# Sending the row maxima from ScalarE's queue, and storing the last chunk in two parts

## The chip, the cores and the metric

The kernel runs on one core of a Trainium2 chip. The metric is the device time of one execution in microseconds (us), lower is better. The engines are called PE (TensorE, matmul), PEld (TensorE's weight load), ACT (ScalarE), DVE (VectorE), POOL (GpSimd) and SP (SyncE). A name with q behind it (SPq, ACTq) stands for an instruction that the engine's own sequencer carries out, such as the issue of a DMA.

## The reference

One sequence of 2048 tokens by 256 features goes through three sublayers. The first and the third are the same attention with 16 heads of 16 features: the queries have 16 heads, but keys and values are those of the one head that a gate picks for each token.

```python
def _L0_ffn_ref(x, W_gate, W_qkv):              # T = 2048, C = 256, H = 16, hd = 16
    gating = softmax(x @ W_gate.T);  idx = argmax(gating)
    indicator = one_hot(idx, H);     gating_top1 = indicator * max(gating)
    q, k, v = split(x @ W_qkv.T, 3)             # k, v as (T, H, hd)
    k_shared = einsum('bth,bthd->btd', indicator, k)
    v_shared = einsum('bth,bthd->btd', gating_top1, v)
    att = einsum('bhqd,bkd->bhqk', q, k_shared) / sqrt(hd)
    att = softmax(where(causal, att, -inf))
    return einsum('bhqk,bkd->bhqd', att, v_shared)
...
x = x + 0.5 * _L0_ffn_ref(_layernorm(x), W_gate, W_qkv)
x = x + recurrence(_layernorm(x))               # gates, a scan over tokens, two projections
x = x + 0.5 * _L0_ffn_ref(_layernorm(x), W_gate, W_qkv)
```

## The kernel before

The tokens are cut into 4 chunks of 512 (QW). An attention sublayer (l = 0 or 1) works on units (l, c, g): one chunk of queries and one group of 4 heads, so 32 units in all. Layer 1 takes its chunks in the order 1, 2, 0, 3. A unit goes over its key tiles of 128 keys; a pair (unit, key tile) is a step.

Before a unit's scores can be made, each query needs the maximum of its scores. PE makes score matmuls for that alone ("max" items, line 1724), and DVE reduces them to mxp (lines 1445 and 1448), in some cases after a relu on ACT (line 1217). DVE joins the maxima into mx2 ("join"). The item "row" then has three parts: PE turns mx2 into rows (line 1715), ACT copies these rows from PSUM to the tile m_row (32 x 128, line 1136), and two DMAs take m_row into two extra rows of the query tile q_t, one for the heads of each parity (line 891). There the maximum is subtracted within the score matmul itself, since the keys have a constant in the matching rows. There are two slots of m_row, with a semaphore s_md for each. The first score matmul of a unit ("qk", line 1746) waits for both DMAs.

A step then is: two pairs of score matmuls on PE ("qk"), an exponential on ACT for each pair (line 1229, 128 x 1024 elements, PSUM to the tile probs), a causal mask on POOL for the diagonal tiles (line 971), and the product with the values on PE ("pv", line 1758). After a unit's last step ACT copies the sums (o_sb, line 1237), PE transposes them (line 1733), DVE divides (lines 1472 and 1476) and POOL adds the result to x_sb (line 977, semaphore s_xa). PSUM has 8 banks; a qk pair takes two, a max item one, a unit's sums one.

What each engine does, and in which order, is one static list ORDER. The function weave makes it from a planner's costs before the program is built, and every engine walks through that list and takes the items that are its own. An engine carries out its items strictly in order; semaphores hold it back where data or a bank isn't ready. Short filler matmuls ("warm", lines 1562 and 1565) are in PE's list where the planner saw a gap.

SP issues the DMAs in the same order of items: "qout" (queries to DRAM, line 868), "qin" (queries back in another layout, line 880), "row" (line 891) and "out" (the store of a finished chunk of layer 1, line 897).

Of the kernel before, what the change touches and what calls it, by code (L numbers as in the profile page):

```python
# [6 lines left out]
D = 256  # L7
# [3 lines left out]
P = 128  # L11
EPS = 1e-5
NT = T // P
QW = 512
NCH = T // QW
TC = QW // P
GH = 4
NG = H // GH
# [27 lines left out]
ROWS_M = [slice(HALF * par + KX, HALF * par + KX + 2) for par in range(2)]  # L46
# [13 lines left out]
UNITS = [(0, c, g) for c in range(NCH) for g in range(NG)] \  # L60
# [172 lines left out]
def unit_no(l, c, g):  # L233
    return UNITS.index((l, c, g))
# [327 lines left out]
FREED, _count = {}, {True: 0, False: 0}  # L562
# [30 lines left out]
def fine(l, c):  # L593

    return (l, c) not in SINGLE
# [5 lines left out]
def exp_no(s, k):  # L601

    return PER_STEP * s + k + 1


def filled(e):
    return FILL_NO[e] + 1


def prep_no(l, c):  # L610
    return NO["keys", l, c]


def macaron_block(nc, x, gamma, beta, w_in, b_in, w_out, b_out, w_skip, b_skip, w_gate, w_qkv, out):
# [6 lines left out]
    with ctx:  # L621
        def sb(name, shape, dt=f32):
            return ctx.enter_context(nc.sbuf_tensor(name, shape, dt))
# [4 lines left out]
        def sem(name):  # L628
            return ctx.enter_context(nc.semaphore(name))
# [88 lines left out]
        q_t = sb("q_t", [P, NCH, DC, GH * QW], f16)  # L718
# [4 lines left out]
        m_row = sb("m_row", [2 * GH * TC, 2, P], f16)  # L723
# [27 lines left out]
        def bank_of(e):  # L751
            return ps[:, BANK[e], :]
# [6 lines left out]
        def as_rows(bank):  # L759
            return bank[0:2 * GH * TC, 0:P // 2].bitcast(f16)  # L760
# [9 lines left out]
        s_md = [sem(f"s_md{i}") for i in range(2)]  # L770
        s_out = sem("s_out")
# [3 lines left out]
        s_ra = sem("s_ra")  # L775

        s_qk = sem("s_qk")
# [4 lines left out]
        s_xa = sem("s_xa")  # L782
# [38 lines left out]
        def bands(c):  # L821
            return x_sb[:, TC * c:TC * c + TC, :]
# [16 lines left out]
        def scores_done(u):  # L839

            return exp_no(LAST[u], PER_STEP - 1)

        @block.sync
        def _(sp):
            sp.dma_start(bands(0)[:, 0:2, :], x[0, 0:2 * P, :].rearrange("(t p) d -> p t d", p=P)).then_inc(s_xld[0], 16)

            sp.wait_ge(s_wqkv, 32)
            for c in range(1, NCH):
                sp.dma_start(bands(c), x[0, c * QW:(c + 1) * QW, :].rearrange("(t p) d -> p t d", p=P))\
                    .then_inc(s_xld[c], 16)  # L850
            sp.dma_start(gamma_c[:, :], gamma.rearrange("(a p) -> p a", p=P),
                         allow_slow_non_contiguous=True).then_inc(s_wcol, 16)
            sp.dma_start(beta_c[:, :], beta.rearrange("(a p) -> p a", p=P),
                         allow_slow_non_contiguous=True).then_inc(s_wcol, 16)
            sp.dma_start(b_in_c[:, :], b_in.rearrange("(a p) -> p a", p=P),
                         allow_slow_non_contiguous=True).then_inc(s_wcol, 16)
            sp.dma_start(w_in_sb[:, :, :], w_in.rearrange("(a p) e -> p a e", p=P)).then_inc(s_wbr, 16)
            sp.dma_start(w_skip_sb[:, :, :], w_skip.rearrange("(a p) e -> p a e", p=P)).then_inc(s_wbr, 16)
            sp.dma_start(w_out_sb[:, :], w_out).then_inc(s_wbr, 16)
            sp.dma_start(b_out_r[:, :], b_out.partition_broadcast(P)).then_inc(s_wrow, 16)  # L860
            sp.dma_start(b_skip_r[:, :], b_skip.partition_broadcast(P)).then_inc(s_wrow, 16)

            for e in ORDER:
                if e[0] == "qout":
                    _, l, c, b = e
                    n = prep_no(l, c)
                    sp.wait_ge(s_rd, FREED["q", l, c, b])
                    sp.dma_start(q_scratch[n, :, b].rearrange("a p t -> p a t"), q_part[:, :, b, :])\
                        .then_inc(s_qw[b], 16)
                elif e[0] == "qin":  # L870
                    _, l, c, b = e
                    n = prep_no(l, c)
                    sp.wait_ge(s_qw[b], 16 * (n + 1))
                    if l:

                        sp.wait_ge(s_qk, scores_done(unit_no(0, c, 2 * b + 1)))
                    for par in range(2):
                        for r, part in enumerate(Q_PART):
                            row = HALF * par + HD * r
                            sp.dma_start(  # L880
                                q_t[row:row + HD, c, b, :].rearrange("p (h t) -> p h t", t=QW),
                                q_scratch[n, part, b].rearrange("(h o d) t -> o d h t", o=2, d=HD)[par],
                            ).then_inc(s_qt[n][b], 16)
                elif e[0] == "row":
                    l, c, g = UNITS[e[1]]
                    sp.wait_ge(s_ra, FREED[e])
                    if l:
                        sp.wait_ge(s_qk, scores_done(unit_no(0, c, g)))
                    for par in range(2):
                        o = g % 2 * 2 * QW  # L890
                        sp.dma_start(q_t[ROWS_M[par], c, g // 2, o:o + 2 * QW],
                                     m_row[GH * TC * par:GH * TC * par + GH * TC, e[1] % 2, :])\
                            .then_inc(s_md[e[1] % 2], 16)
                elif e[0] == "out":
                    c = e[1]
                    sp.wait_ge(s_xa, unit_no(1, c, NG - 1) + 1)
                    sp.dma_start(out[0, c * QW:(c + 1) * QW, :].rearrange("(t p) d -> p t d", p=P),
                                 bands(c)).then_inc(s_out, 16)
            sp.wait_ge(s_out, 16 * NCH)

        @block.gpsimd
        def _(pool):
# [16 lines left out]
            def stats_of(e):  # L919
                _, l, c = e  # L920
                k = NO[e]
                pool.wait_ge(s_var, k + 1)
                if k:

                    pool.wait_ge(s_ln, k)
                own(g_.tensor_tensor(rstd[:, :], var[:, :], half[:, 0:TC], op=ALU.pow))  # L926
                g_.tensor_tensor(shift[:, :], neg[:, :], rstd[:, :], op=ALU.mult).then_inc(s_std, 1)

            def norm(e):
                _, l, c = e  # L930
                k = NO[e]
                pool.wait_ge(s_std, k + 1)
                if k:

                    pool.wait_ge(s_fill, filled(TURNS[k - 1]))
                for t in range(TC):
                    last = g_.tensor_scalar(u[:, t, :], x_sb[:, TC * c + t, :], rstd[:, t:t + 1], shift[:, t:t + 1],  # L937
                                            ALU.mult, ALU.add)
                last.then_inc(s_ln, 1)
# [165 lines left out]
        def _(act):  # L1105
# [6 lines left out]
            def evict(e):  # L1112

                bank = bank_of(e)
                act.wait_ge(s_fill, filled(e))
                if e[0] == "wgate":
                    a_.activation(wg_t[:, :, :], bank[:, 0:DC * H].rearrange("p (a h) -> p a h", a=DC), ACT.Copy)\
                        .then_inc(s_ra, 1)
                elif e[0] == "turn" and fine(e[1], e[2]):
                    dst = u2t_x if e[1] == 2 else ut_x  # L1120
                    a_.activation(dst[:, e[3], :, :].rearrange("p a t -> p (a t)"), bank[:, :].bitcast(f16), ACT.Copy)\
                        .then_inc(s_ra, 1)
                elif e[0] == "turn":
                    a_.activation(ut[:, e[3], :], bank[:, :], ACT.Copy).then_inc(s_ra, 1)
                elif e[0] == "keys":
                    _, l, c = e
                    a_.activation(k_tl[:, l, c, :], bank[:, 0:QW // 2].bitcast(f16), ACT.Copy).then_inc(s_ra, 1)  # L1127
                elif e[0] == "dkeys":
                    to = (kd_tl if e[2] else kh_tl)[:, e[1], :]
                    n = to.shape[1]  # L1130
                    a_.activation(to, bank[:, 0:n // 2].bitcast(f16), ACT.Copy).then_inc(s_ra, 1)
                elif e[0] == "row":
                    v = e[1]
                    if v >= 2:
                        act.wait_ge(s_md[v % 2], 32 * (v // 2))
                    a_.activation(m_row[:, v % 2, :], as_rows(bank), ACT.Copy).then_inc(s_ra, 1)

            def preparation(e):
                kind, l, c = e[0], e[1], e[2]
# [668 lines left out]
```

## Time and profile before

| | |
|---|---|
| median of 2 runs | 888.76 us (886.53 to 891.0) |
| profiled execution, its own time | 891.59 us |
| its span, first to last instruction | 889.9 us |
| PE, DVE, ACT, POOL busy | 95%, 84%, 81%, 33% of the span |
| mean granted clock of TensorE | 0.974 of full speed |
| row DMAs (line 891) | 64, of 4.0 KB each |
| chunk stores (line 897) | 4, of 512 KB each, 2.9 us from issue to landing |

The 1.69 us between the profiled execution's own time and its span lie before the first and behind the last instruction. An idle share of an engine says little here by itself, since the engines hand work to each other in one static order.

### The profile page before, as it was taken

Reading aid. Unit: us, or ns where it says so; the run is one execution under the profiler, and the core shown is the slowest. Engines: PE = TensorE matmul, PEld = TensorE weight load, DVE = VectorE, ACT = ScalarE, POOL = GpSimd, SP = SyncE. Lnnn points to the kernel's source line nnn. Section 1 sums busy time; section 2 is a strip of 40 time slices with the busy share of each in tenths; the row PEclk is TensorE's granted clock in tenths of the full one; section 3 lists DMA queues with packets and bytes.
Section 4 is the critical chain, followed back from the end, with each engine's and each line's share of the span. In section 5 each row is a group of like instructions: output and inputs, shape, how many; then the busy total and the mean of one; then the engine's idle time right before and its main releaser. Section 6 shows DMA issues by size and latency. Waiting matters only on the chain.

```text
span 889.9 us, 19042 instructions
## 1 busy us (share of the span) xinstructions
PE 844.8 (95%) x6460; PEld 291.6 (33%) x6460; DVE 747.1 (84%) x2379; ACT 720.6 (81%) x1169; POOL 295.7 (33%) x568
## 2 busy tenths in 40 slices
PE   9898999999999999999999999999999999999997
PEld 6433423332222332324233433342223323222221
DVE  5898778999999989887945889999998999999920
ACT  1148677868998788888979887889998788999996
POOL 3225404633104415046355445632113424110110
PEclk9899689999999999999999999999999999999999
DMA  6110000110000000100010002000001000000000
GB/s 189 49 43 19 2 2 5 57 43 20 1 2 2 1 1 1 43 18 3 1 53 9 2 2 61 3 1 26 1 1 39 25 25 3 24 3 1 2 1 24
DMA packets 20256, 18.03 MB, mean 20 GB/s; under 512 B 4144, under 2 KB 20160, under 8 KB 20160
## 3 DMA queue, kind: packets, MB, share of 16 engines
q1 hardware_dynamic: 19072, 15.74, 5.8%
q8 instruction: 53, 0.87, 0.4%
q10 hardware_dynamic: 1088, 1.07, 0.4%
q14 instruction: 43, 0.35, 0.1%
HBM read 10.24 MB, written 6.29 MB: 19 GB/s over the span
## 4 chain that ended last, share of the span: by engine, by line
PE 59%; DVE 18%; issue 9%; ACT 9%; POOL 5%; DMA 0%; POOLq 0%; SPq 0%; ACTq 0%; DVEq 0%
PE ps L1758 20%; PE ps L1724 12%; PE ps L1746 11%; DVE ps L1448 7%; DVE mxp L1445 5%; ACT probs L1229 5%; PE ps L1642 3%; ACT relu L1217 2%; PE ps L1690 2%; DVE mxp L1448 2%; PE ps L1657 2%; PE ps L1647 2%; PE ps L1565 1%; POOL u L937 1%; POOL u_x L986 1%
## 5 line engine op out<-in xcount | busy, mean ns | idle before, releaser
L1229 ACT ACTIVATE probs<-ps 128x1024 f32<-128x1024 f32 (+5 forms) x802 | 554.9, 767 | 81.2 <-PE ps L1746 76.3
L1758 PE MATMUL ps<-probs,v_l 128*32 128x512 f32 (+3 forms) x2560 | 301.9, 549 | 2.9 <-DVE mxp L1445 0.6
L1448 DVE CUSTOM_DVE_ANT_0 ps<-ps,mask 128x384 f32<-128x384 f32 (+3 forms) x512 | 234.2, 524 | 28.7 <-PE ps L1724 26.7
L1746 PE MATMUL ps<-q_t,k_tl 50*128 50x512 f16 (+3 forms) x1280 | 240.0, 356 | 14.4 <-ACT probs L1229 3.9
L1445 DVE TENSOR_REDUCE mxp<-ps 128x1 f32<-128x512 f32 x384 | 240.2, 683 | 12.7 <-PE ps L1724 10.1
L1724 PE MATMUL ps<-k_tl,q_t 48*128 48x512 f16 (+3 forms) x1152 | 239.4, 340 | 6.9 <-ACT k_tl L1127 1.9
L971 POOL TENSOR_SCALAR_AFFINE_SELECT probs<-probs 128x256 f32<-128x256 f32 x256 | 102.1, 411 | 396.4 <-ACT probs L1229 394.6
L1448 DVE CUSTOM_DVE_ANT_0 ps<-ps,relu 128x256 f32<-128x256 f32 (+1 forms) x256 | 136.1, 586 | 16.3 <-PE ps L1724 15.4
L1724 PEld LDWEIGHTS ps<-k_tl,q_t 48*128 48x128 f16 x1152 | 74.8, 95 | 158.9 <-DVE mxp L1445 48.1
L1746 PEld LDWEIGHTS ps<-q_t,k_tl 50*128 50x128 f16 x1280 | 65.6, 94 | 182.3 <-ACT probs L1229 85.3
L1217 ACT ACTIVATE relu<-ps 128x512 f32<-128x512 f32 x192 | 106.8, 621 | 5.7 <-PE ps L1724 5.2
L1448 DVE DVE_READ_ACCUMULATOR2_ANT mxp<- 128x1 f32 x768 | 108.0, 141 | 0.0
L1758 PEld LDWEIGHTS ps<-probs,v_l 128*32 128x32 f32 x2560 | 53.0, 108 | 86.2 <-issue 69.4
L999 POOL TENSOR_TENSOR prod<-prod 128x512 f32<-128x512 f32 (+2 forms) x42 | 34.5, 821 | 19.3 <-DVE prod L1408 17.1
L1472 DVE RECIPROCAL rec<-ps 128x16 f32<-128x16 f32 x32 | 8.0, 251 | 36.2 <-PE ps L1733 34.8
L1724 PE MATMUL ps<-kd_tl,q_t 48*128 48x512 f16 x128 | 36.3, 382 | 1.6 <-DVE gd L1381 0.5
L977 POOL TENSOR_TENSOR x_sb<-x_sb,y_att 128x256 f32<-128x256 f32 x32 | 23.3, 729 | 43.4 <-DVE y_att L1476 43.3
L1642 PE MATMUL ps<-wqkv_x,ut_x 128*128 128x512 f16 x144 | 34.6, 380 | 0.0
L926 POOL TENSOR_TENSOR rstd<-var,half 128x4 f32<-128x4 f32 x12 | 12.5, 1038 | 59.9 <-DVE neg L1293 59.9
L1408 DVE TENSOR_TENSOR prod<-ps,pick 128x512 f32<-128x512 f32 x32 | 21.9, 687 | 7.1 <-PE ps L1642 5.6
L937 POOL TENSOR_SCALAR u<-x_sb,rstd,shift 128x256 f32<-128x256 f32 x48 | 26.0, 559 | 1.1
L986 POOL TENSOR_TENSOR u_x<-u,u_x 128x512 f16<-128x512 f32 x20 | 23.2, 1160 | 1.7
(182 smaller groups left out, 633.2 us busy)
## 6 DMA issues: line engine op xcount, KB each, us to landing
q_t<-q_scratch SPq DMA_DIRECT2D x96, 64.0 KB, 2.2
q_scratch<-q_part SPq DMA_DIRECT2D x16, 256.0 KB, 2.2
out_dram<-x_sb SPq DMA_DIRECT2D x4, 512.0 KB, 2.9
x_sb<-in_L_attn_x_dram SPq DMA_DIRECT2D x3, 512.0 KB, 5.1
q_t<-m_row SPq DMA_DIRECT2D x64, 4.0 KB
wqkv_n<-in_L_ffn_W_qkv_dram ACTq DMA_DIRECT2D x1, 768.0 KB, 5.5
w_in_sb<-in_L_attn_W_in_dram SPq DMA_DIRECT2D x1, 384.0 KB, 5.5
x_sb<-in_L_attn_x_dram ACTq DMA_DIRECT2D x1, 256.0 KB, 3.5
```

The lines of the kernel that those rows point to most:

```text
L937: last = g_.tensor_scalar(u[:, t, :], x_sb[:, TC * c + t, :], rstd[:, t:t + 1], shift[:, t:t + 1], ALU.mult, ALU.add)
L971: g_.affine_select(out=pr, in_=pr, compare_op=ALU.is_ge, fill=0.0, base=0, pattern=[[0, 2], [1, P]], channel_multiplier=-1).then_inc(s_msk, 1)
L986: g_.tensor_tensor(u_x[:, 1, :, dc * P:(dc + 1) * P], whole, first, op=ALU.subtract).then_inc(s_half, 1)
L999: own(g_.tensor_tensor(pairs[:, :, 0:m], pairs[:, :, 0:m], pairs[:, :, m:2 * m], op=ALU.add))
L1217: a_.activation(relu[:, n % RELU_BUFS, :], bank_of(e), ACT.Relu).then_inc(s_ra, 1)
L1229: last = a_.activation(out if len(banks) == 1 else out[:, n:n + 1, :], bank[:, :, P * i:QW], ACT.Exp, scale=SCALE / LIFT ** 2)
L1445: last = v_.tensor_reduce(to, scores, axis=AX, op=ALU.max)
L1448: last = v_.tensor_tensor_reduce(scores, scores, added, 1.0, LOWEST, ALU.add, ALU.max, accum_out=to)
L1642: last = mm(bank[:, :], ut_x[:, dc, a, t * P:(t + 1) * P], wqkv_x[:, b, dc, D:3 * D], start=n == 0, stop=n == 3 * DC - 1)
L1724: last = mm(bank[:, col:col + w], q_rows(ROWS_X, c, g, hh, i * P, P), keys, start=True, stop=True)
L1746: last = mm(ps[:, BANK[e][n], P * i:QW], k_cols(ROWS_XM, hh, l, kt, P), q_rows(ROWS_XM, c, g, hh, P * i, QW - P * i), start=True, stop=True)
L1758: last = mm(out_bank[VW * hh:VW * hh + VW, P * i:QW], v_l[:, l, kt, :], probs[:, s % NB, hh, P * i:QW], start=j == 0, stop=j == key_tiles( ...
```

## The change

Two things change. First, the row DMAs leave SP's list: ACT, right after its copy into m_row, waits for that copy to be complete (s_ra) and in layer 1 for the layer-0 scores of the same chunk and heads (s_qk), and issues the same two DMAs itself. Second, the store of the last chunk goes out in two DMAs: columns 0 to 191 once the third group of heads has been added, columns 192 to 255 once the fourth has. The other three stores stay whole. ORDER and every other instruction stay the same.

```diff
-                elif e[0] == "row":
-                    l, c, g = UNITS[e[1]]
-                    sp.wait_ge(s_ra, FREED[e])
-                    if l:
-                        sp.wait_ge(s_qk, scores_done(unit_no(0, c, g)))
-                    for par in range(2):
-                        o = g % 2 * 2 * QW
-                        sp.dma_start(q_t[ROWS_M[par], c, g // 2, o:o + 2 * QW],
-                                     m_row[GH * TC * par:GH * TC * par + GH * TC, e[1] % 2, :])\
-                            .then_inc(s_md[e[1] % 2], 16)
                 elif e[0] == "out":
+
                     c = e[1]
-                    sp.wait_ge(s_xa, unit_no(1, c, NG - 1) + 1)
-                    sp.dma_start(out[0, c * QW:(c + 1) * QW, :].rearrange("(t p) d -> p t d", p=P),
-                                 bands(c)).then_inc(s_out, 16)
-            sp.wait_ge(s_out, 16 * NCH)
+                    w = D // NG
+                    for cols in [slice(0, D)] if c != UNITS[-1][1] else [slice(0, D - w), slice(D - w, D)]:
+                        sp.wait_ge(s_xa, unit_no(1, c, cols.stop // w - 1) + 1)
+                        sp.dma_start(out[0, c * QW:(c + 1) * QW, cols].rearrange("(t p) d -> p t d", p=P),
+                                     bands(c)[:, :, cols]).then_inc(s_out, 16)
+            sp.wait_ge(s_out, 16 * (NCH + 1))
...
                     a_.activation(m_row[:, v % 2, :], as_rows(bank), ACT.Copy).then_inc(s_ra, 1)
+                    l, c, g = UNITS[v]
+                    act.wait_ge(s_ra, FREED[e])
+                    if l:
+                        act.wait_ge(s_qk, scores_done(unit_no(0, c, g)))
+                    for par in range(2):
+                        o = g % 2 * 2 * QW
+                        act.dma_start(q_t[ROWS_M[par], c, g // 2, o:o + 2 * QW],
+                                      m_row[GH * TC * par:GH * TC * par + GH * TC, v % 2, :])\
+                            .then_inc(s_md[v % 2], 16)
```

On ACT, around the last of the 32 rows, this stood before (probs are the exponentials, o_sb the sums of the unit before):

```order
L1229 ACTIVATE probs<-ps 128x1024 x18
L1136 ACTIVATE m_row<-ps 32x128
L1229 ACTIVATE probs<-ps 128x1024 x2
L1229 ACTIVATE probs<-ps 128x512 x2
L1229 ACTIVATE probs<-ps 128x1024 x2
L1237 ACTIVATE o_sb<-ps 128x512
```

And this stands there now; the line numbers of later code have moved by two, those of the row by seven:

```order
L1231 ACTIVATE probs<-ps 128x1024 x18
L1129 ACTIVATE m_row<-ps 32x128
L1136 DMA q_t<-m_row 2x8x128 x2
L1231 ACTIVATE probs<-ps 128x1024 x2
L1231 ACTIVATE probs<-ps 128x512 x2
L1231 ACTIVATE probs<-ps 128x1024 x2
L1239 ACTIVATE o_sb<-ps 128x512
```

The two DMAs stand between the copy and the next exponentials, and so it is at all 32 rows.

At the end of SP's list this stood before:

```order
L891 DMA q_t<-m_row 2x8x128 x4
L897 DMA out_dram<-x_sb 128x4x256
L891 DMA q_t<-m_row 2x8x128 x2
L897 DMA out_dram<-x_sb 128x4x256
L891 DMA q_t<-m_row 2x8x128 x6
L897 DMA out_dram<-x_sb 128x4x256
```

And now:

```order
L880 DMA q_t<-q_scratch 16x4x512 x6
L890 DMA out_dram<-x_sb 128x4x256 x2
L890 DMA out_dram<-x_sb 128x4x192
L890 DMA out_dram<-x_sb 128x4x64
```

SP is left with the query trips and the stores, and the last store has become two.

## Rows read from the trace of the kernel before

**Rows 1.** The page: busy times, then the chain that ended last.

```profile
PE 844.8 (95%) x6460; PEld 291.6 (33%) x6460; DVE 747.1 (84%) x2379; ACT 720.6 (81%) x1169; POOL 295.7 (33%) x568
...
PE 59%; DVE 18%; issue 9%; ACT 9%; POOL 5%; DMA 0%; POOLq 0%; SPq 0%; ACTq 0%; DVEq 0%
```

**Rows 2.** Busy times in the 10 us behind a row: 21 rows with little idle ACT.

```profile
core 0: us, PE busy (x) PEld busy (x) DVE busy (x) ACT busy (x) POOL busy (x), PEclk, DMA share, GB/s
...
227.97:237.97 10.00, 9.49 (x69) 2.57 (x67) 9.31 (x39) 9.93 (x17) 0.00 (x0) 1.00 0.01 2
...
277.85:287.85 10.00, 8.66 (x68) 2.40 (x68) 9.71 (x46) 9.88 (x18) 5.73 (x9) 1.00 0.00 1
317.26:327.26 10.00, 10.00 (x80) 4.38 (x80) 7.68 (x27) 9.70 (x16) 1.29 (x1) 1.00 0.01 2
...
640.98:650.98 10.00, 9.75 (x69) 2.76 (x67) 10.00 (x41) 9.65 (x16) 0.00 (x0) 1.00 0.01 2
...
sum 210.00, PE 197.09 PEld 64.94 DVE 188.55 ACT 198.92 POOL 67.35; mean PE 9.39 PEld 3.09 DVE 8.98 ACT 9.47 POOL 3.21
```

**Rows 3.** The same behind the other 11 rows.

```profile
42.28:52.28 10.00, 9.84 (x29) 4.07 (x26) 9.64 (x42) 1.71 (x2) 0.42 (x1) 0.70 0.00 1
...
495.02:505.02 10.00, 10.00 (x88) 5.09 (x86) 8.07 (x28) 8.24 (x14) 2.20 (x2) 1.00 0.01 3
...
sum 110.00, PE 102.91 PEld 39.44 DVE 91.15 ACT 72.87 POOL 32.17; mean PE 9.36 PEld 3.59 DVE 8.29 ACT 6.62 POOL 2.92
```

**Rows 4.** By tile m_row: durations in ns (min/median/max), then who waited for it.

```profile
L891 SPq DMA_DIRECT2D q_t<-m_row x64: 598/612/818, 42.3 to 851.8; - x64
L1136 ACT ACTIVATE m_row<-ps x32: 250/256/268, 42.0 to 850.8; 32x128 f16<-32x128 f16 x32
...
  PE ps L1746: 1.7, 1
```

**Rows 5.** Timeline at the last row, ACT and SP: start, length, what.

```profile
850.85 0.27 ACT L1136 ACTIVATE m_row<-ps 32x128 f16<-32x128 f16 x1
851.14 1.27 SPq L891 DMA_DIRECT2D q_t<-m_row  x2
851.17 2.92 ACT L1229 ACTIVATE probs<-ps 128x1024 f32<-128x1024 f32 x4
```

**Rows 6.** Timeline of the program's start, SP's queue and ACT.

```profile
0.79 0.44 SPq L845 DMA_DIRECT2D x_sb<-in_L_attn_x_dram  x1
...
0.79 0.48 ACTq L1107 DMA_DIRECT2D x_sb<-in_L_attn_x_dram  x1
...
1.83 0.56 ACTq L1110 DMA_DIRECT2D wg_n<-in_L_ffn_W_gate_dram  x1
2.43 1.28 ACT L1117 ACT_TABLE_LOAD   x1 [2.43 <-issue]
```

**Rows 7.** Timeline of ACT and PEld behind the rows at 317 and 817 us.

```profile
317.30 1.94 ACT L1229 ACTIVATE probs<-ps 128x1024 f32<-128x1024 f32 x2
...
319.45 0.16 PEld L1758 LDWEIGHTS ps<-probs,v_l 128*32 128x32 f32 x8 [0.43 <-ACT probs L1229]
...
817.28 1.94 ACT L1229 ACTIVATE probs<-ps 128x1024 f32<-128x1024 f32 x2
...
818.86 0.09 PEld L1724 LDWEIGHTS ps<-k_tl,q_t 48*128 48x128 f16 x1 [0.84 <-ACT probs L1229]
```

**Rows 8.** Timeline of the one unit whose first scores waited for the row.

```profile
92.35 1.25 SPq L891 DMA_DIRECT2D q_t<-m_row  x2
...
94.85 0.39 PE L1746 MATMUL ps<-q_t,k_tl 50*128 50x512 f16 x2 [1.69 <-DMA q_t<-m_row]
```

**Rows 9.** Timeline of SP's queue at the second row.

```profile
54.52 1.26 SPq L891 DMA_DIRECT2D q_t<-m_row  x2
55.82 1.33 SPq L880 DMA_DIRECT2D q_t<-q_scratch  x2
```

**Rows 10.** The page's DMA issues: count, KB each, median us to landing.

```profile
q_t<-q_scratch SPq DMA_DIRECT2D x96, 64.0 KB, 2.2
q_scratch<-q_part SPq DMA_DIRECT2D x16, 256.0 KB, 2.2
out_dram<-x_sb SPq DMA_DIRECT2D x4, 512.0 KB, 2.9
```

**Rows 11.** Timeline of the program's end.

```profile
859.31 0.73 POOL L977 TENSOR_TENSOR x_sb<-x_sb,y_att 128x256 f32<-128x256 f32 x1
...
885.80 0.72 POOL L977 TENSOR_TENSOR x_sb<-x_sb,y_att 128x256 f32<-128x256 f32 x1 [24.68 <-DVE y_att L1476]
886.55 0.38 SPq L897 DMA_DIRECT2D out_dram<-x_sb  x1
```

## The prediction, made before the changed kernel ran

> **What bounds the kernel now.** I read the page's busy times first, then the chain that ended last, then the surroundings of each of the 32 row items, since that is where the change puts its work. PE is busy 95% of the span, DVE 84%, ACT 81%, and the chain that ended last lies on PE for 59%, on DVE for 18% and on ACT for 9% [rows 1]. By these shares ACT has 169 us of idle time (889.9 less 720.6), and 64 more instructions on it would look harmless. The reader should not stop there. Busy shares are averages, and ACT's idle time lies mostly early in the program. So I took the 10 us that follow the end of each copy into m_row and asked how long ACT is busy in them. In 21 of the 32 ACT is idle for less than 1.3 us; together it is busy 198.92 of 210 us there, so it has 0.53 us to spare per window, while PE and DVE are busy 9.39 and 8.98 of 10 us [rows 2]. In the other 11 it has 3.4 us to spare (110 less 72.87, by 11) [rows 3]. Behind most rows, then, three engines run close to full in one static order, and no single one is "the" bound: PE waits for a bank that ACT or DVE frees, and ACT waits for scores of PE.
>
> **The change, part by part: the move of the row DMAs.** It adds to ACT, per row, a wait for its own copy and two DMA issues, and takes the same two issues from SP. How long is ACT away from its exponentials? On SP an issue of this transfer takes 0.612 us in the median [rows 4], and the two together 1.27 us from the first's start to the second's end [rows 5]. Is it the same on ACT? The trace of before has no row DMA on ACT, but at the program's start both queues issue a load of x_sb of one shape, at the same moment: 0.44 us on SP, 0.48 us on ACT [rows 6]. I scale by that: 1.27 x 0.48 / 0.44 = 1.39 us, with 1.27 us as the lower end. Does the issue block ACT's compute? After its third load, which runs to 2.39 us, ACT's next instruction starts at 2.43 us, and not before [rows 6]; so I take the issue as blocking, and the other reading as a rival below. The wait for its own copy costs little: SP, which waits for the same semaphore, starts 0.02 us after the copy's end, and the next exponential started 0.05 us after it anyway [rows 5]. The additional layer-1 wait is for scores of layer 0 that were made long before, so it costs nothing. Sum: ACT is away for about 1.37 us per row (0.02 + 1.39 + 0.04 for the restart, less some 0.08 that it lay idle or overlapped anyway), and 32 x 1.37 = 44 us in all. What is queued behind each is the exponentials of the steps in progress; PE waits for these, for the banks and for probs, and DVE waits for PE's max items.
>
> **What of it reaches the end.** Nothing in the trace shows a pause of this length put into ACT, so I bound it. The lower end of one row's price is 0 (its cover is ACT's idle time), the upper end 1.37 us. Between them I read how much later an exponential could have ended before PE noticed. Behind the row at 317 us two exponentials end at 319.24 us, and PE's next product starts at 319.45 us, released by ACT: a margin of 0.2 us. Behind the row at 817 us the first of two ends at about 818.25 us (half of 1.94 us after 817.28), and PE's next item that ACT releases starts at 818.86 us: 0.6 us [rows 7]. So 1.37 us on ACT arrive on PE as 0.8 to 1.15 us. Part of that is given back later. In 9 of the 21 tight windows DVE is busy 9.7 us or more of 10, as at 277.85 and 640.98 us [rows 2]: there PE has waits on DVE that shrink when it comes late, and DVE works on banks that are filled already. In the other 12, as at 317.26 us with PE busy for the whole window and DVE for 7.68 us [rows 2], I see nothing that gives it back. I choose 1.0 us for these 12, 0.6 us for the 9, and 0.4 us for the 11 loose rows, in which ACT has 3.4 us to catch up but PE may still be held at once (at 495.02 us PE has no idle time at all) [rows 3]. These three prices are my choice between the ends, the first by the 0.8 to 1.15 us read above. Sum: 12 + 5.4 + 4.4 = 21.8 us.
>
> **Does the move win anything?** A row would gain if SP had kept it waiting. It did not: at the last row SP starts 0.02 us after the copy's end [rows 5], and at each of the other 31 it is 0.02 or 0.03 us as well. The path of the row itself, from the copy to the first scores, was waited for just once, for 1.7 us in the whole run [rows 4], behind a row whose DMAs started at 92.35 us and let the scores start at 94.85 us, 2.50 us later [rows 8]. Issued by ACT the trip is the same or 0.1 us longer. Query trips no longer stand behind rows in SP's queue (behind the second row they did, for 1.3 us) [rows 9], but no instruction of the trace waits for a query trip, so that is worth nothing. What SP loses was free.
>
> The Trainium skill has a rule that speaks otherwise of the price: its page "DMA: Bandwidth & Descriptors", section "Issuing engines are not separate DMA queues", says that all issuing engines feed the same 16 DMA engines, and that using several saves only the sequencer's time for the start, "which is usually small relative to the DMA itself". Its first half agrees with the paragraph above: nothing is won at the DMA engines. By its second half the issue on ACT would be near nothing, and the whole change would come out at the -0.5 us of the store. Here the trace does not agree: two issues take 1.27 us of a trip of 2.50 us, and the engine that pays is one that others wait for.
>
> **The last store.** Now POOL ends its last addition at 886.52 us, SP issues the store at 886.55 us [rows 11], and 2.9 us later the 512 KB have landed [rows 10]. In the changed kernel 384 KB can go as soon as the third group is added, at about 860 us [rows 11], some 26 us earlier, hidden by the last unit. What is left is 128 KB in rows of 256 bytes. Its landing time has no row; the nearest are the 256 KB and 64 KB transfers at 2.2 us each [rows 10], which say that the part that doesn't shrink is most of it. So the gain is about 0.7 us if it lands in 2.2 us, and 0 if short rows cost what fewer bytes save; I take 0.5 us. The first part's issue and its wait stand on SP, where nothing else is queued by then.
>
> **The sum.** +21.8 - 0.5 = +21.3 us. The profiled execution took 891.59 us, with 889.9 us of span and 1.69 us around it; it would become 912.9 us. It lay 2.8 us above the median of the two runs. Against the median of 888.76 us the forecast is 910.1 us.
>
> **The rivals.** (a) Absorbed. ACT catches up in its idle time, the delay seldom reaches a full PE, and rows cost 0.1 to 0.4 us. For it: ACT is idle 169 us in all, and DVE seldom waits for PE. Against it: the margins of 0.2 and 0.6 us [rows 7]. At 0.25 us per row it gives 8 - 0.5 = +7.5, so 896 us. (b) Paid in full, or more: each pause passes whole through the loop from ACT to PE and back, 44 - 0.5 = +43, so 932 us; it would be more if TensorE's clock fell in further stretches, as it did to 0.70 behind the first row [rows 3]. Against it: there is some margin at each place that I read. (c) The issue doesn't block ACT's compute, since it is the sequencer's own work and activations already handed over go on. The pauses are then mostly gone and the store's 0.5 us remain: 888.3 us, no change. Against it: ACT's first compute instruction waited until the loads were issued [rows 6]. (d) The other side, faster: SP's queue is the hidden brake, in that a row trip issued at once on ACT lets the next unit begin earlier. It would decide if the trip were waited for often; at 1.7 us in the whole run its ceiling, with the store, is 1.7 + 0.7 = 2.4 us, so 886.4 us. A gain of over 2% has no mechanism that I can find, so it keeps only what I may have overlooked. That the change doesn't do what it says is not a case: the order of instructions shows the DMAs on ACT at all 32 rows.
>
> **Chances.** The forecast, rows at 0.5 to 0.9 us on average, 0.57; absorbed 0.18; in full or more 0.13; no blocking 0.08; faster by little or much 0.04. For the range, the forecast's own case reaches from 903 to 919 us. To hold 8 times in 10 I go down to 894 us, which takes in most of the absorbed case, and up to 932 us, the full price. Two per cent, 17.8 us, is about what a measurement of this kernel can tell from no change; it puts the border at 906.5 us, inside the forecast's own case, whose larger part lies above it (0.42 of its 0.57). With the full case that makes slower 0.57; within 2% 0.40, and faster by over 2% 0.03.
>
> **What would show it.** Right: the row DMAs of ACT's queue last 0.6 to 0.7 us each; the exponential behind a row starts some 1.4 us after the copy's end instead of 0.05; ACT's busy time stays near 720 us while the span grows; the waits of PEld for ACT's exponentials grow; the last store lands in 2.2 to 2.6 us. Wrong: exponentials run on during the issues (rival c); the delay seen behind a row is gone 20 us later (rival a); PE's clock shows new dips (rival b). The prediction rests most on the three prices per row, which I chose and could not read.

## The result, and the profile after

The changed kernel took 920.12 us in the median (919.58 to 920.65), against 888.76 us before: a ratio of 1.0353, with a 95% interval of 1.0238 to 1.0468. That is slower by 31.4 us, where 21.3 us was forecast (910.1 us, range 894 to 932). Its profiled execution took 919.58 us, with a span of 917.8 us.

The page first. These are its busy times and the chain that ended last; before, they were [rows 1].

```profile
PE 849.3 (93%) x6460; PEld 290.5 (32%) x6460; DVE 749.0 (82%) x2379; ACT 718.9 (78%) x1169; POOL 295.3 (32%) x568
...
PE 56%; ACT 15%; DVE 12%; issue 11%; ACTq 3%; POOL 2%; DMA 0%; POOLq 0%; DVEq 0%
```

The reader should see that no engine got more work: ACT's busy time is 1.7 us lower, DVE's 1.9 us and PE's 4.5 us higher, where the span grew by 27.9 us. ACT's share of the chain has gone from 9% to 15%, and ACTq, the DMA issues themselves, from 0% to 3%. The span grew by idle time, and the list of waits says whose. Its columns: who waited for whom, total us, times, longest.

```profile
PEld ps L1748 <- ACT probs L1231: 100.0, 184, 2.0
...
DVE ps L1450 <- PE ps L1726: 65.6, 68, 8.5
PEld ps L1726 <- ACT probs L1231: 60.6, 99, 2.1
```

Before, these three were 85.3, 42.1 and 43.9 us, so PE waits more for ACT's exponentials, and DVE more for PE's max items. This is the timeline of the changed kernel at the last row, at the same place as [rows 5].

```profile
879.05 0.27 ACT L1129 ACTIVATE m_row<-ps 32x128 f16<-32x128 f16 x1
879.35 1.27 ACTq L1136 DMA_DIRECT2D q_t<-m_row  x2
...
880.67 2.43 ACT L1231 ACTIVATE probs<-ps 128x1024 f32<-128x1024 f32 x3 [1.35 <-PE ps L1748]
881.74 0.16 PEld L1760 LDWEIGHTS ps<-probs,v_l 128*32 128x32 f32 x8 [1.50 <-ACT probs L1231]
```

The next exponential starts 1.35 us after the copy's end, not 0.05 us, and 0.05 us after the second issue. It is so behind 31 of the 32 rows, and the median gap is 1.38 us; behind the first row ACT lay idle for 6.1 us in both kernels. In some places ACT had been idle for a while before as well, so the 32 gaps together grew by 37.8 us, 1.18 us per row. The view names PE as what ended that idle time, but the scores had been ready since before 880 us; what held ACT were its own two issues. The row's trip is unchanged: one unit still waits for it, 1.7 us in all, as in [rows 4].

Next, the windows of 10 us behind three of the rows. In [rows 2] they began at 227.97, 277.85 and 640.98 us.

```profile
core 0: us, PE busy (x) PEld busy (x) DVE busy (x) ACT busy (x) POOL busy (x), PEclk, DMA share, GB/s
228.47:238.47 10.00, 8.89 (x63) 2.43 (x61) 8.32 (x37) 8.59 (x16) 0.00 (x0) 1.00 0.01 2
280.96:290.96 10.00, 8.42 (x56) 1.87 (x52) 7.41 (x37) 7.48 (x13) 5.73 (x9) 0.83 0.00 1
658.70:668.70 10.00, 9.00 (x65) 2.60 (x63) 9.07 (x37) 8.42 (x14) 0.00 (x0) 1.00 0.01 2
```

Behind the first, ACT is busy 8.59 us instead of 9.93, 1.34 us less, and has caught up nothing within 10 us; DVE has lost 0.99 us too. The third is the window at 640.98 us in [rows 2], where DVE had been busy for all of its 10 us: it is down to 9.07. The second shows something more. TensorE's granted clock is 0.83 there, where it was 1.00 before. What such a dip costs can be read at this very place, since a later run, with the same rows on ACT and the old store, had none here. This is the stretch from this copy's end to the next row's copy's end, in the kernel before, in the changed one and in that run.

```profile
277.85:317.28 39.43, 37.50 (x275) 11.77 (x271) 38.09 (x108) 33.28 (x54) 17.06 (x27) 1.00 0.01 1
```

```profile
280.96:322.82 41.86, 39.00 (x275) 11.89 (x271) 38.21 (x108) 33.32 (x54) 17.02 (x27) 0.96 0.01 1
```

```profile
289.05:329.69 40.64, 37.75 (x275) 11.72 (x271) 38.23 (x108) 33.20 (x54) 17.08 (x27) 1.00 0.01 1
```

The same work took 1.2 us more at a clock of 1.00, which is the pause, and 2.4 us more with the dip. Just before the dip PE had stood still for 0.98 us, waiting for the exponential behind the issues; it did so in the later run as well, where no dip followed. Of the 31 stretches from one row's copy to the next, nine have a lower mean clock than before, by 0.04 to 0.16. They are 1.6 to 2.5 us longer, the others at most 1.4 us (but for one that has a dip in both kernels). The clock gave a piece back too: this is one stretch of each kernel, first before, then changed, between the same two rows or nearly so.

```profile
100.00:150.00 50.00, 47.81 (x354) 17.03 (x349) 39.12 (x164) 35.90 (x62) 16.01 (x28) 0.80 0.01 2
```

```profile
105.00:148.00 43.00, 38.88 (x350) 15.20 (x350) 38.81 (x164) 35.67 (x62) 15.92 (x28) 0.99 0.01 2
```

The same work took about 7 us less at a clock of 0.99 than at 0.80. So in this profiled execution the first rows had put the kernel 5.1 us behind (the copy at 92.06 us came at 97.13), a faster clock then brought it to 0.8 us ahead (168.99, now 168.16), and from there to the last row's copy (850.85, now 879.05) it lost 29.0 us in 24 rows. Over the whole execution the mean clock came out about even, 0.976 against 0.974, and that looks like chance: the long time at a low clock behind 92 us is in the traces of most runs, that of the rows alone among them.

Last, the end of the program, as in [rows 11].

```profile
914.74 0.72 POOL L970 TENSOR_TENSOR x_sb<-x_sb,y_att 128x256 f32<-128x256 f32 x1 [24.69 <-DVE y_att L1478]
915.49 0.37 SPq L890 DMA_DIRECT2D out_dram<-x_sb  x1
```

From the last issue to the end of the span it is 2.3 us (917.8 less 915.49), before it was 3.35 us (889.9 less 886.55): the split store gives 1.0 us. Of the loss of 27.9 us in span, 28.9 us stood at the last store's issue already.

### The profile page after: what moved, and what is told of

The parts are those of the page before. It is cut to its first block, busy times and chain, and to the rows that moved or that the text cites. A ratio compares the mean times of both kernels' runs of the same rounds, so it can differ in the third digit from the quotient of the medians.

```text
span 917.8 us, 19043 instructions
## 1 busy us (share of the span) xinstructions
PE 849.3 (93%) x6460; PEld 290.5 (32%) x6460; DVE 749.0 (82%) x2379; ACT 718.9 (78%) x1169; POOL 295.3 (32%) x568
## 4 chain that ended last, share of the span: by engine, by line
PE 56%; ACT 15%; DVE 12%; issue 11%; ACTq 3%; POOL 2%; DMA 0%; POOLq 0%; DVEq 0%
PE ps L1760 19%; PE ps L1726 12%; ACT probs L1231 10%; PE ps L1748 10%; DVE ps L1450 5%; DVE mxp L1447 4%; ACTq L1136 3%; PE ps L1644 3%; ACT relu L1219 2%; PE ps L1649 2%; PE ps L1692 2%; PE ps L1659 2%; DVE mxp L1450 1%; PE ps L1564 1%; PE ps L1664 1%
## 5 line engine op out<-in xcount | busy, mean ns | idle before, releaser
L1239 ACT ACTIVATE o_sb<-ps 128x512 f32<-128x512 f32 x32 | 20.0, 624 | 7.3 <-PE ps L1760 4.3
```

## The experiments

Each run was timed beside runs of the kernel before on the same chip; "us above before" is the ratio less one, times the median of these, 890 to 892 us. The theory is that ACT's absence from its exponentials is the whole loss. The rivals are a share of the store, the empty queue of ACT that comes with the wait, the row's trip, and something in DMA issues as such.

**The two halves of the change.** The store alone: SP keeps the rows, and only the last chunk's store goes in two.

```diff
-                    sp.wait_ge(s_xa, unit_no(1, c, NG - 1) + 1)
-                    sp.dma_start(out[0, c * QW:(c + 1) * QW, :]...
+                    for cols in [slice(0, D)] if c != UNITS[-1][1] else [slice(0, D - w), slice(D - w, D)]:
+                        sp.wait_ge(s_xa, unit_no(1, c, cols.stop // w - 1) + 1)
+                        sp.dma_start(out[0, c * QW:(c + 1) * QW, cols]...
```

> The rows stay with SP, and only the last store goes in two parts. In the changed kernel the last part took 2.0 us to land where the whole store took 2.9 us. The pause theory (all of the loss comes from the two issues on ACT) expects 0.9 us less than before, 887.9 us, ratio 0.999. The rival that the split store has a share in the loss (its longer landing, its wait) expects more than before, by 1 us or more. A measurement of 5 rounds may not tell 0.9 us from nothing; the time from POOL's last addition to the end of the span can.

Measured: 0.9992 (0.9970 to 1.0015), 12 runs. That is no difference that a time can show. The trace can:

```profile
885.28 0.72 POOL L980 TENSOR_TENSOR x_sb<-x_sb,y_att 128x256 f32<-128x256 f32 x1 [24.68 <-DVE y_att L1479]
886.03 0.37 SPq L900 DMA_DIRECT2D out_dram<-x_sb  x1
```

With a span of 888.4 us, the end comes 2.4 us after the last issue, 1.0 us sooner than before. The rows alone, with the store whole:

```diff
-                elif e[0] == "row":                # in SP's list
...
+                    act.wait_ge(s_ra, FREED[e])    # in ACT's, behind the copy into m_row
...
+                    for par in range(2):
+                        act.dma_start(q_t[ROWS_M[par], ...
```

> The rows are issued by ACT, and the store stays whole. The pause theory expects the changed kernel's time plus 0.9 us, that is about 921 us, 32 us above before. The rival that the store has a share expects clearly less than 920 us.

Measured: 1.0414 (1.0368 to 1.0459), 36.9 us above before. The rows carry all of the loss. It is more than the expected 32 us, but the interval of the changed kernel's own ratio takes it in. The clock is the likely rest: these executions ran at a mean of 0.963 to 0.970. The fastest, 923.17 us at 0.970, is 30 us above those of the kernel before at 0.970 (892.98 to 893.51 us); and the changed kernel's 919.58 us at 0.976 is 28 to 29 us above those at 0.976 (890.42 to 891.5 us).

**What about the two issues costs?** First the wait alone, with SP issuing as before:

```diff
                     a_.activation(m_row[:, v % 2, :], as_rows(bank), ACT.Copy).then_inc(s_ra, 1)
+                    act.wait_ge(s_ra, FREED[e])
+                    act.sem_inc(s_own, 1)
```

> SP issues all row DMAs as before, but ACT waits behind each copy until it is complete, and adds one to a semaphore of its own. Pause theory: the wait alone costs what the sequencer needs to go on, 0.1 to 0.2 us per row, of which at most half reaches the end: 0 to +4 us, 889 to 893 us. The rival that the emptied queue of ACT (it can no longer hand over the next activation while one runs) is the main cost expects half of the loss or more: +15 us or more.

Measured: 1.0016 (1.0000 to 1.0032), 1.4 us. The gap behind the copy goes from 0.06 to 0.17 us in the median. By themselves the wait and the emptied queue are not the cause. Then one of the two DMAs on ACT, the other on SP at the same time:

```diff
+                    for par in (0,):
+                        act.dma_start(q_t[ROWS_M[par], ...
-                    for par in range(2):
+                    for par in (1,):
                         sp.dma_start(q_t[ROWS_M[par], ...
```

> ACT issues the first of a row's two DMAs, SP the second, at the same time. ACT is away for about 0.7 us instead of 1.37. If nothing of a pause is absorbed, half of the loss: +15 to +16 us, 904 us. If each row has a fixed margin of 0.2 to 0.6 us that is used up first, less: +3 to +10 us, 892 to 899 us. If the loss were in the trip of the row's data through ACT's queue rather than in ACT's pause, the first scores would wait the same, and nearly all of it would stay.

Measured: 1.0138 (1.0097 to 1.0179), 12.3 us, between the two expectations. This is ACT at the last row:

```profile
860.05 0.27 ACT L1136 ACTIVATE m_row<-ps 32x128 f16<-32x128 f16 x1
860.35 0.65 ACTq L1143 DMA_DIRECT2D q_t<-m_row  x1
861.04 3.83 ACT L1238 ACTIVATE probs<-ps 128x1024 f32<-128x1024 f32 x5 [0.72 <-PE ps L1755]
```

The median gap is 0.72 us, so half of the pause costs a third of the loss (12.3 of 36.9 us). It isn't the trip: the data still goes by ACT's queue in part, and as early. Now the same pause without a DMA, made of compute that nobody uses:

```diff
+                    act.wait_ge(s_pad, 3 + v)
+                    a_.activation(pad_to[:, :, :, :], pad[:, :, :].unsqueeze(1).to_broadcast([P, 4, 3, P]),
+                                  ACT.Copy).then_inc(s_pad, 1)
```

> SP issues all row DMAs as before, and ACT makes one additional copy of 128 x 1536 elements from one spare tile to another behind each copy into m_row, which nobody uses. It should last 1.3 to 1.5 us. Pause theory: the same loss as with the DMAs, +28 to +36 us, 917 to 925 us, since only ACT's absence counts. If the DMA issue as such hurts (the queue, the emptied pipeline, contention with SP), clearly less, +20 us or below.

Measured: 1.0345 (1.0328 to 1.0362), 30.7 us.

```profile
878.33 0.27 ACT L1143 ACTIVATE m_row<-ps 32x128 f16<-32x128 f16 x1
878.50 1.47 ACT L1145 ACTIVATE pad_to<-pad 128x1536 f32<-128x1536 f32 x1
879.87 4.67 ACT L1239 ACTIVATE probs<-ps 128x1024 f32<-128x1024 f32 x6
```

From the copy's start to the next exponential it is 1.54 us here, 1.62 us in the changed kernel and 0.32 us before [rows 5]. Over all rows the pauses grew by 34.2 us, with the DMAs by 37.8 us. The right comparison is with the rows alone, where the store is whole as well: 30.7 us (29.2 to 32.3) against 36.9 us (32.8 to 40.9). So most of the loss is ACT's time, whatever fills it. Of the difference of 6.2 us, 3.6 us is the shorter pause; the rest is near the edge of the two intervals and stays open. At last the issues doubled, with two more DMAs of the same data to a spare tile:

```diff
+                    for par in range(2):
+                        act.dma_start(spare[ROWS_M[par], v % 2, :],
+                                      m_row[GH * TC * par:GH * TC * par + GH * TC, v % 2, :])\
+                            .then_inc(s_sp[v % 2], 16)
```

> As the changed kernel, and ACT issues two more DMAs of the same m_row to a spare tile, so that it is away for 2.65 us per row. With no margin, the second 1.27 us costs like the first: twice the loss, +63 us, 952 us. With a margin of 0.2 to 0.6 us per row that the first pair has used up, the second costs its whole length, 32 x 1.27 = 41 us on top: 961 us. If the delay is absorbed in part in any case, less than +60 us.

Measured: 1.12 (1.1161 to 1.1239), 106.8 us, more than any expectation, at a mean granted clock of 0.925 in the profiled execution (before 0.974).

```profile
953.69 1.27 ACTq L1143 DMA_DIRECT2D spare<-m_row  x2
955.01 3.83 ACT L1238 ACTIVATE probs<-ps 128x1024 f32<-128x1024 f32 x5 [2.67 <-issue]
956.08 0.16 PEld L1769 LDWEIGHTS ps<-probs,v_l 128*32 128x32 f32 x8 [2.83 <-ACT probs L1238]
956.08 1.15 PE L1769 MATMUL ps<-probs,v_l 128*32 128x512 f32 x8 [2.33 <-ACT probs L1238]
```

PE stands still for 2.33 us there. The granted clock from 200 us on was 0.94 in this run and 0.99 before, that is, it fell to the lower level (1.2 GHz) more often. ACT's gaps grew by 77.8 us in all, so at least 29 us of the 106.8 us are no pause. An estimate fits that: executions of the kernel before took 886.3 to 887.2 us at a mean clock of 0.981 or 0.982 and 893.0 to 893.5 us at 0.970, some 6.6 us for 0.012, which makes about 32 us for the fall from 0.977 to the 0.92 of these four.

**Where do rows cost?** The rows were given to ACT in groups, by the windows of the kernel before; the others stayed with SP.

```diff
+LOOSE = (0, 1, 2, 4, 5, 6, 15, 16, 20, 24, 25)    # units; BY_ACT in the later two runs
...
+                    if v not in LOOSE:
+                        ...                       # ACT issues, as in the changed kernel
...
-                elif e[0] == "row":
+                elif e[0] == "row" and not (e[1] not in LOOSE):
```

> ACT issues the DMAs of the 21 rows behind which ACT is idle for less than 1.3 of 10 us; SP issues those of the other 11. If ACT's idle time nearby is the cover (the forecast's grading of 1.0 and 0.6 against 0.4 us), most of the loss stays. From the shifts of the rows between the two traces, 1.3 us per tight row: +27 us, about 916 us. If every row costs the same wherever it stands (0.98 us, 31.4 us by 32): +21 us, 909 us. By the forecast's own prices, +17 us, 906 us.

> ACT issues the DMAs of the 11 loose rows only, SP the other 21. Cover theory: what the tight rows leave, 0.4 to 0.7 us each: +4 to +8 us, 893 to 897 us. Equal prices: +11 us, 900 us. If PE is held at once and nothing is given back, 1.37 us each: +15 us, 904 us.

> ACT issues the DMAs of the 9 tight rows behind which DVE is busy 9.7 us or more of 10; SP issues those of the other 23. The forecast gave these rows 0.6 us each, since DVE's backlog should give part of the delay back: +5.4 us, 896 us. If nothing is given back beyond a margin of 0.3 us, 1.05 us each: +9.5 us, 900 us. By the shifts of the rows between the two traces, 1.3 us each: +11.5 us, 902 us.

> ACT issues the DMAs of the other 12 tight rows; SP issues those of the remaining 20. The forecast gave 1.0 us each: +12 us, 902 us. If DVE's backlog matters, clearly more per row than in the run with the 9. If it doesn't, the same per row, 1.05 to 1.4 us: +13 to +17 us, 903 to 907 us.

Measured, per row with the interval of the ratio carried over:

| rows on ACT | ratio (95% interval) | us above before | us per row | forecast |
|---|---|---|---|---|
| 21 tight | 1.0367 (1.0305 to 1.0428) | 32.7 | 1.56 (1.29 to 1.81) | 0.83 |
| 11 loose | 1.0112 (1.0059 to 1.0165) | 10.0 | 0.91 (0.48 to 1.34) | 0.4 |
| 9 tight, DVE full | 1.0108 (1.0067 to 1.0149) | 9.6 | 1.07 (0.66 to 1.48) | 0.6 |
| 12 other tight | 1.0210 (1.0187 to 1.0233) | 18.7 | 1.56 (1.39 to 1.73) | 1.0 |

Rows cost more where ACT had less to spare, and more where DVE was not full, in the order of the forecast; but both pairs of intervals touch or overlap, so the order is likely rather than shown. What is plain is the level: every group costs 1.6 to 2.3 times its forecast. The two halves add up (32.7 + 10.0 = 42.7 against 36.9 us, within their intervals).

The level has two causes, though. For the 12 rows it is no less than the pause itself (1.56 us, where the gaps grow by 1.42 us in the mean), and that leaves no room for the margins that the table below shows. The executions show what does: those with the loose rows took 892.78 and 893.86 us at mean clocks of 0.980 and 0.978, and 901.96 and 903.41 us at 0.965 and 0.961. Set beside executions of the kernel before within 0.001 of their clock, the 11 loose rows cost 3 to 6 us, the 9 rows 10 to 13 us and the 12 rows (those at 0.971 and 0.969) 14 to 16 us. Per row that is some 0.4, 1.3 and 1.3 us: an estimate, from few executions, in which a full DVE gives nothing back.

The traces say how a single pause is paid. This table has rows behind which the clock was 1.00 up to the next row. The pause is the time from the copy's start to ACT's next compute instruction, the stretch the time to the start of the next row's copy; both are given as their growth over the kernel before, in us, and a margin is what the pause grew more than the stretch.

| row (copy's end before) | one issue: pause, stretch | two issues: pause, stretch | four issues: pause, stretch | margin, two issues |
|---|---|---|---|---|
| 227.97 | 0.68, 0.60 | 1.34, 1.26 | lower clock | 0.08 |
| 317.26 | 0.69, 0.57 | 1.35, 1.23 | 2.65, 2.53 | 0.12 |
| 541.59 | 0.56, 0.34 | 1.23, 1.01 | 2.54, 2.32 | 0.22 |
| 817.32 | 0.80, 0.44 | 1.77, 1.42 | lower clock | 0.35 |
| 400.63 | 0.75, -0.03 | 1.40, 0.62 | lower clock | 0.78 |
| 665.68 | 0.66, -0.02 | 1.31, 0.48 | lower clock | 0.83 |

Each place has a margin of its own, from nearly 0 to 0.8 us, and what is above it is paid one for one, for one issue, for two and for four. Of the 31 stretches, 16 had a clock of 1.00 in both kernels. Among them are 6 of the 9 rows with a full DVE, at 0.9 to 1.4 us (mean 1.18), 6 of the 12, at 0.5 to 1.35 us (mean 1.04), and 4 of the 11 loose ones, at 0 to 0.7 us (mean 0.30).

**Does another engine or another place pay less?** POOL issues all rows; the store goes in two parts.

```diff
+                elif e[0] == "row":               # in POOL's list, taken from SP's
+                    pool.wait_ge(s_ra, FREED[e])
...
+                        pool.dma_start(q_t[ROWS_M[par], ...
```

> POOL, the least busy compute engine (33%), issues the row DMAs; the store goes in two parts. If it is only ACT's place in the loop of PE and ACT that makes the pause dear, POOL's pause costs little: 0 to +5 us, 889 to 895 us. If every compute engine pays, because POOL's masks on the diagonal tiles and its share of the norms stand behind the issues, +10 us or more. The row's trip may also be longer from POOL's queue; then first scores wait for it.

Measured: 1.0121 (1.0055 to 1.0186), 10.8 us: a third of ACT's price, at an engine that is busy 33% of the time. Its rows by tile:

```profile
L1101 POOL DMA_DIRECT2D q_t<-m_row x64: 561/574/775, 41.9 to 864.9; - x64
...
  PE ps L1749: 6.4, 6
```

The issue takes 0.57 us. Six units now wait for their row, 6.4 us in all, instead of one for 1.7 us. In the trace four stretches carry most of the loss: behind the rows at 403, 458, 525 and 864 us (400, 451, 515 and 851 before) they are 3.3, 3.6, 4.0 and 2.7 us longer, while the span grew by 15.6 us; the first three have a clock of 0.89 to 0.96, where it was 1.00. Five rows also left POOL 1.1 to 3.8 us after the copy, the others 0.3 to 0.4 us. What POOL's late masks cost apart from the late rows stays open. The last run keeps both issues on ACT, but the second of a row only behind the next two exponentials:

```diff
+                    send(v, 0)
+                    later.append([v, 0])           # send(v, 1) two "qk" items later
```

> As the changed kernel, but ACT issues only a row's first DMA behind the copy, and the second behind the next two exponentials. The same 64 issues, in two pauses of 0.66 us. If each pause has a margin of its own of about 0.3 us, as the run with one of the two DMAs suggests (+12 us for 32 pauses of 0.66 us): twice 12, +24 us, 914 us. If the price goes by the total time on ACT, no difference from the changed kernel: 920 to 926 us. If the second DMA comes too late for the next unit's first scores, more than that, and the trace shows waits for it.

Measured: 1.0247 (1.0213 to 1.0280), 22.0 us, and the wait for late rows had grown:

```profile
PE ps L1760 <- DMA q_t<-m_row: 7.9, 4, 3.5
```

That is near the +24 us expected for two short pauses per row, but the trace shows that there aren't two. This is ACT at the row before the last:

```profile
837.38 0.26 ACT L1143 ACTIVATE m_row<-ps 32x128 f16<-32x128 f16 x1
837.67 0.62 ACTq L1110 DMA_DIRECT2D q_t<-m_row  x1
838.69 1.94 ACT L1242 ACTIVATE probs<-ps 128x1024 f32<-128x1024 f32 x2 [1.05 <-PE ps L1760]
840.41 0.65 ACTq L1110 DMA_DIRECT2D q_t<-m_row  x1
840.51 1.09 ACT L1230 ACTIVATE relu<-ps 128x512 f32<-128x512 f32 x2
```

The second issue starts while an exponential runs, and the relu behind it starts 0.10 us into the issue, without idle time. All 32 second issues start under a running instruction, and behind 27 of them ACT has no idle time at all. So they cost ACT nothing; the stretches behind the rows at 227.97 and 317.26 us grow by 0.60 and 0.58 us, as with one of the two DMAs (0.60 and 0.57). Its span is 15.7 us longer than that run's (914.9 against 899.2 us), and 14.8 us of this lie in three stretches, in which the first scores waited 3.5, 2.5 and 1.7 us for the late row and the clock was 0.87 to 0.96.

This sharpens what the changed kernel shows. There the issues stand right behind a wait for ACT's own copy, so ACT has nothing else handed to it while they last. The wait alone lengthened the gap by 0.1 us, and an issue under a running instruction cost nothing; by these runs it is the two together that make a pause of 1.38 us. A run with both DMAs at the later place, or with the wait taken away, was not made.

## Why the prediction was right, and where its sizes were not

**The pause: nearly right.** 1.37 us per row was forecast as what comes on top, 44 us in all. Measured, the median gap is 1.38 us, of which 0.06 us was there before; all gaps together grew by 37.8 us. An issue on ACT takes 0.62 us, hardly more than SP's 0.61 us, so scaling by the load at the start [rows 6] overstated it, and more of the pause fell into time that ACT lay idle anyway than the 0.08 us of the forecast. That the issue blocks the compute behind it holds for this place, behind a wait for ACT's own result. The rival of a non-blocking issue (c) fell for the changed kernel, but what it says of activations already handed over is what the second issues of the spread run did, all 32 of them. The Trainium skill's page "Perfetto Trace Analysis", section "DMA Instruction — HWDGE (DVE, Sync)", says of a DMA's reported window that it ends when the sequencer is free for the next instruction. The changed kernel's trace agrees, with 0.05 us between the issue's end and the next exponential.

**No gain from a faster start: right.** The one wait for a row stayed at 1.7 us. The Trainium skill's page "DMA: Bandwidth & Descriptors", section "Issuing engines are not separate DMA queues", calls the time to start a DMA usually small beside the DMA, and by that there would have been no change; the run with the rows alone, at 1.0414, speaks against it for this kernel.

**A margin per row: right as a mechanism.** The forecast read margins of 0.2 and 0.6 us from [rows 7] and let 0.8 to 1.15 us of a pause arrive at PE. The table above has the same two places, the rows at 317 and 817 us: their margins were 0.12 and 0.35 us, so both readings were too large, but a fixed margin at each place, with the rest paid, is what the traces show. Over the 16 stretches at full clock the mean margin is 0.33 us.

**Given back later: wrong for a full DVE, and this is the term that was mis-sized.** The forecast took 0.6 us for the 9 rows with a full DVE, because of its backlog. At full clock they cost 1.18 us in the mean, as much as the rows without such a backlog. In the trace a full DVE loses 0.93 us of its 10 us at once, so its backlog covers little of a pause of this length. The other two prices held at full clock: 1.04 us where 1.0 was forecast, and 0.30 us where 0.4 was. Rival (b), every pause in full, would have given 43 us by the forecast's pauses; by those measured it is 37.8 us. The absorbed case (a), with the pauses costing 7.5 us, is refuted by the rows alone.

**The clock: named, but not priced.** This is the second term that was missing. The forecast had dips of the clock only as an aggravation of rival (b) and gave "PE's clock shows new dips" as a sign of being wrong. The sign came: nine stretches of the changed kernel have a lower clock than before. Four of these (behind 145.72, 277.85, 357.17 and 515.15 us) ran at full clock with the rows alone and were 1.2 to 1.5 us shorter there, so a dip of this size about doubles what a pause costs. The dips came with the pauses, but not at the same places in every execution. That the measured 920.12 us lies within the range, and so near the forecast's own case (903 to 919 us), owes something to luck: two terms were too small, and the long time at a low clock near 100 us, which the kernel before had, was missing in the profiled execution. That the clock makes the difference between the changed kernel's 31.4 us and the 36.9 us of the rows alone fits the executions at equal clock given above, but was not tested by itself, and the intervals of the two overlap.

**One sum of the chances.** 0.42 of the forecast's own case and 0.13 of the full price make 0.55 for a slowdown of over 2%, not 0.57.

**The store: right in sign.** 0.5 us was forecast and 1.0 us gained, as the last 128 KB land in 2.0 us and not in the 2.4 us that the 0.5 us stood for.

## What to carry to other kernels

An engine's idle share doesn't tell whether it can spare time for a DMA issue; only the microseconds around the very place do. Right behind a wait for the engine's own last result, an issue keeps the compute behind it back for its whole length (0.62 us each here); issued while an instruction already runs, it cost ACT nothing. But later is not free either: the row that left later let the next unit's scores wait. In a loop in which three engines hand work to each other in a fixed order, each place has a small margin (here 0 to 0.8 us), what is above it is paid in full, and a pause that lets PE stand still can cost as much again by a lower clock. A version that beats the kernel before by more than its noise was not found; the split store alone is 1.0 us better in the trace, and its time can't be told from the old one.

## What the runs showed of the hardware that was not expected

The landing time of a store split by columns doesn't follow its bytes. These rows are from the page of the changed kernel (count, KB each, median us to landing).

```profile
out_dram<-x_sb SPq DMA_DIRECT2D x3, 512.0 KB, 3.3
...
out_dram<-x_sb SPq DMA_DIRECT2D x1, 384.0 KB, 4.6
```

384 KB in pieces of 768 bytes took 4.6 us, longer than the whole 512 KB in pieces of 1 KB (3.3 us here, 2.9 us before [rows 10]), while 128 KB in pieces of 256 bytes took 2.0 us. Here the long one is hidden by the last unit. With the store alone split, the 384 KB took 4.7 us; with the rows on POOL, with the issues doubled and with them spread, 2.6 us, in the same pieces. So the length of the pieces doesn't explain it, and it stays open.

The issue of a 4 KB transfer between two tiles costs more of the sequencer's time (0.61 us on SP, 0.62 on ACT, 0.57 on POOL) than that of 256 KB from q_part to DRAM (0.38 us on SP).
